# First layer's x loaded a second time in turned form, its low part made by GpSimd; the gate term c turned from a column of v; new placement numbers

## The reference

```python
# layer 0
q, k, v = (proj(Wq, bq), proj(Wk, bk), proj(Wv, bv))
scores = where(adj + eye > 0, q @ k^T / sqrt(32), -inf)
h = x + softmax(scores) @ v @ Wo.T + bo
x = layer_norm(h)
# layer 1
a = x @ w_g[:D];  c = x @ w_g[D:]
scores = Q @ K^T / sqrt(32) + a[:, :, None] + c[:, None, :] + b_g + log(adj + 1e-9)
x = softmax(scores) @ V + x
# layer 2
f = x @ W_fc + b_fc;  logits = leaky(f @ w_q + (f @ w_k)^T + (1 - adj) * -1e9)
x = softmax(logits) @ f + x
# layer 3: as layer 0, with log(max(adj, 1e-8)) added to the scores
```

## Time and profile before

| | before |
|---|---|
| median of 3 runs | 1841.64 us |
| profiled execution | 1840.3 us |
| its span | 1838.4 us |
| TensorE (PE) busy | 1731.4 us (94%), 23564 matmuls |
| VectorE (DVE) busy | 1483.9 us (81%) |
| ScalarE (ACT) busy | 1214.8 us (66%) |
| GpSimd (POOL) busy | 1269.3 us (69%) |
| DMA | 66.46 MB, mean 36 GB/s |
| chain that ended last | PE 77%, DVE 17%, ACT 2% of the span |

### The profile page before, as it was taken

One profiled execution on the slowest core, in us unless ns is written; L12 is line 12 of the kernel. 1 busy time (PEld: TensorE's weight loads), 2 busy tenths in 40 slices (PEclk: granted clock), 3 DMA queues, 4 the chain that ended last, 5 costly groups with the idle time before them and its releaser, 6 DMA issues.

```text
span 1838.4 us, 54870 instructions
## 1 busy us (share of the span) xinstructions
PE 1731.4 (94%) x23564; PEld 1321.4 (72%) x23564; DVE 1483.9 (81%) x3008; ACT 1214.8 (66%) x1894; POOL 1269.3 (69%) x903
## 2 busy tenths in 40 slices
PE   5999998899999999889999999989999999998996
PEld 4677776777777777677777777767777777767774
DVE  5899877777799977877789987787779998777775
ACT  3567765567777676456776777546777676754675
POOL 4443898288964489638895459945888446992788
PEclk8999999999999999999999999999999999999998
DMA  6100010001120000100221000010112100011011
GB/s 166 36 30 13 19 37 25 24 25 53 49 75 19 19 19 31 47 2 25 60 75 43 24 19 19 25 46 8 42 53 71 42 19 18 15 36 35 14 30 36
DMA packets 67734, 66.46 MB, mean 36 GB/s; under 512 B 6051, under 2 KB 67493, under 8 KB 67493
## 3 DMA queue, kind: packets, MB, share of 16 engines
q1 hardware_dynamic: 66388, 62.16, 11.3%
q10 hardware_dynamic: 1104, 0.79, 0.1%
HBM read 54.54 MB, written 8.39 MB: 34 GB/s over the span
## 4 chain that ended last, share of the span: by engine, by line
PE 77%; DVE 17%; ACT 2%; issue 1%; POOL 1%; SPq 1%; DMA 1%; DVEq 0%; POOLq 0%; ACTq 0%
PE gx L609 23%; PE od L747 17%; PE sc L714 17%; PE gx L760 6%; PE gx L634 3%; PE sc L708 3%; PE sc L720 3%; DVE ring L999 3%; PE gx L796 3%; DVE qk L950 2%; PE gx L727 2%; DVE lg L1043 2%; DVE negm L972 1%; DVE parts L972 1%; DVE parts L975 1%
## 5 line engine op out<-in xcount | busy, mean ns | idle before, releaser
L594 POOL TENSOR_TENSOR ring<-ring,adj_c 128x1024 f32<-128x1024 f32 x256 | 609.4, 2406 | 107.7 <-ACT ring L865 55.1
L714 PE MATMUL sc<-qk 32*128 32x256 f32 x9216 | 410.8, 294 | 11.0 <-ACT m_rows L853 4.4
L714 PEld LDWEIGHTS sc<-qk 32*128 32x128 f32 x9216 | 320.5, 184 | 109.3 <-issue 62.7
L850 ACT ACTIVATE aside<-sc 128x1024 f32<-128x1024 f32 x192 | 196.6, 1024 | 232.4 <-PE sc L714 152.7
L865 ACT ACTIVATE ring<-sc 128x1024 f32<-128x1024 f32 x256 | 248.4, 1023 | 29.8 <-PE sc L720 29.3
L569 POOL TENSOR_TENSOR xs<-xs,bo 128x512 f32<-128x512 f32 x96 | 128.3, 1337 | 182.7 <-DVE xt_lo L942 163.5
L747 PE MATMUL od<-ring,vf 128*32 128x256 f32 x3072 | 243.9, 389 | 3.1 <-POOL ring L594 3.1
L747 PE MATMUL od<-ring,ones_r 128*32 128x256 f32 x3072 | 236.7, 380 | 0.0
L972 DVE TENSOR_REDUCE parts<-sc 128x4 f32<-128x1024 f32 x128 | 155.8, 1217 | 50.2 <-PE sc L714 49.5
L999 DVE TENSOR_TENSOR ring<-ring,adj_c 128x1024 f32<-128x1024 f32 x128 | 177.6, 1429 | 0.0
L863 ACT ACTIVATE ring<-sc,vf 128x1024 f32<-128x1024 f32 x128 | 135.8, 1113 | 36.5 <-PE sc L720 36.4
(11 more groups left out here) (146 smaller groups left out, 4433.5 us busy)
## 6 DMA issues: line engine op xcount, KB each, us to landing
adj_c<-in_adj_t SPq DMA_DIRECT2D x96, 256.0 KB, 2.8
adj_r<-in_adj SPq DMA_DIRECT2D x64, 256.0 KB, 3.0
xs<-in_x SPq DMA_DIRECT2D x32, 256.0 KB, 3.1
out<-xs SPq DMA_DIRECT2D x32, 256.0 KB, 2.2
wo<-in_w_o SPq DMA_DIRECT2D x2, 256.0 KB
ring<-in_w_q ACTq DMA_DIRECT2D x1, 256.0 KB, 3.8
ring<-in_w_k ACTq DMA_DIRECT2D x1, 256.0 KB, 4.3
ring<-in_w_v ACTq DMA_DIRECT2D x1, 256.0 KB, 4.6
```

What stands on the lines that cost most here:

```text
L594: pool.tensor_tensor(part, part, adj_c[i.mi % 3][:, t, :].unsqueeze(1).to_broadcast([P, G, N]), ALU.mult).then_inc(weighted, 1)
L714: mm = pe.matmul(sc[:, g, t * N:(t + 1) * N], buf[rows, a, c, t * P:(t + 1) * P], buf[rows, b, c, :], start=(n == 0 and not masked), stop= ...
L850: act.activation(aside[:], sc[:, 0:2, :], ACT.Copy).then_inc(set_aside, 1)
```

## The change

1. **x turned by DMA, layer 0 only.** The host passes `x_t`, the transpose of x. SyncE loads it into two buffers `x_raw` (stage `LT`, 256 KB an item). ScalarE makes `xt_hi` from it, and **GpSimd** makes `xt_lo` = `x_raw` - `xt_hi` (stage `T` in GpSimd's list). The four transposes on TensorE and the subtraction on VectorE are gone in layer 0. x itself is still loaded, for the residual. `XB` of layer 0 now waits for x alone, not for the split.
2. **c from v's column.** GpSimd's `O` now first copies column 257 of v, rounded, and the remainder, into a zeroed `c_pad` (two 128 x 8 instructions). TensorE turns it by two 128 x 128 products with the identity (stage `O`, shaped as `M`), ScalarE copies it to `c_rows`. Gone: six products on TensorE, one VectorE instruction, and the constants `cr_hi`, `cr_lo`, `row_sel`. Scores of item i now wait for V of item i.
3. **New numbers in all tables.** `GAT_START` and `LAST_START` also change, but the order of items stays as it was. `od[0]` and `od[1]` stay two regions.

In the diff the blocks stand in the order SyncE, GpSimd (`T` and `O`), TensorE (`P`, then `O`), ScalarE (`T`).

```diff
 MHA_PLAN1 = {
-    "O": {POOL: [3.4]},
+    "O": {PE: [3.263], ACTE: [3.322], POOL: [-1.904]},
...
-    "P": {PE: [0.888], ACTE: [1.261], DVE: [0.856]},
+    "P": {PE: [0.72], ACTE: [0.977], DVE: [0.737]},
...
+        def x_split(i):
+            return (x0_lo_set, i.i0 + 1) if i.l == 0 else (xt_lo_set, i.k + 1 - i.i0)
...
-            sp.dma_start(xs[:, 0], x_all[items_l0[0].batch]).then_inc(x_loaded[0], 16)
+            sp.dma_start(x_raw[0][:], x_t_all[items_l0[0].batch]).then_inc(xt_loaded[0], 16)
...
+            sp.dma_start(x_raw[1][:], x_t_all[items_l0[1].batch]).then_inc(xt_loaded[1], 16)
             for s, i, c in order[SP]:
-                if s == "LX":
-                    if i.k == 0:
-                        continue
+                if s == "LT" and i.i0 >= 2:
+                    sp.wait_ge(*x_split(items_l0[i.i0 - 2]))
+                    sp.dma_start(x_raw[i.i0 % 2][:], x_t_all[i.batch]).then_inc(xt_loaded[i.i0 % 2], 16)
+                elif s == "LX":
...
+                elif s == "T":
+                    pool.wait_ge(xt_hi_set, i.k + 1)
+                    pool.tensor_tensor(xt_lo[i.k % 2][:], x_raw[i.i0 % 2][:], xt_hi[i.k % 2][:].bitcast(F32), ALU.subtract)\
+                        .then_inc(x0_lo_set, 1)
                 elif s == "O":
+                    gate_c = vf[i.mi % NVF][:, :, D + 1:D + 2].to_broadcast([P, T, G])
+                    pad = c_pad[i.i1 % 2][:].rearrange("p t (g r) -> p t g r", g=G)
                     pool.wait_ge(v_set, v_count(i))
...
+                    pool.tensor_copy(pad[:, :, :, 0], gate_c).then_inc(c_hi_set, 1)
+                    pool.wait_ge(c_hi_set, i.i1 + 1)
+                    pool.tensor_tensor(pad[:, :, :, 1], gate_c, pad[:, :, :, 0].bitcast(F32), ALU.subtract).then_inc(c_pad_set, 1)
...
-                    if s == "P" and i.l == 1:
-                        project(gx_of("ca", i)[:, 0:N], [lambda h: cr_hi[:, h, :], lambda h: cr_lo[:, h, :]],
-                                [lambda h: xh[:, h, :], lambda h: xl[:, h, :]]).then_inc(gx_sem("ca", i), 1)
+                elif s == "O":
+                    pe.wait_ge(c_pad_set, i.i1 + 1)
+                    pe.wait_ge(*gx_emptied("ca", i))
+                    for n in range(T):
+                        mm = pe.matmul(gx_of("ca", i)[:, n * P:(n + 1) * P], c_pad[i.i1 % 2][:, n, :], ident_r[:], start=True, stop=True)
+                    mm.then_inc(gx_sem("ca", i), 1)
...
+                    if i.l == 0:
+                        act.wait_ge(xt_loaded[i.i0 % 2], 16 * (i.i0 // 2 + 1))
+                        if i.k >= 2:
+                            j = items[i.k - 2]
+                            what = "fp1" if j.l == GAT else "vb" if j.l == 1 else "v"
+                            act.wait_ge(gx_sem(what, j), gx_count(what, j))
+                        act.activation(hi, x_raw[i.i0 % 2][:].rearrange("p c n -> p (c n)"), ACT.Copy).then_inc(xt_hi_set, 1)
```

239 lines of the change are left out of this document (113 added, 126 removed).

## The result

The change made the kernel slower: 1895.95 us in the median of 4 runs (1884.13 to 1902.43), beside 1841.02 us (1839.77 to 1842.42) for the kernel before. The ratio is 1.029, 95% interval 1.024 to 1.034. The forecast of 1818 us was wrong in sign, and the loss is larger than that of any rival (C reached to 1879). The profiled execution took 1884.13 us, 43.8 more than the 1840.3 of before, and is the fastest of the four. It also has the highest granted clock, 0.979; the others, at 0.965 to 0.973, took 10 to 18 us more.

A forecast was written before the change was run, and what follows sets the result against it. The prediction took TensorE, busy 94%, as the bound, with VectorE close behind in layer 0 and GpSimd in layer 1. Terms summing to -23.2 took 1840.3 to 1817, and the median's 1.3 gave 1818 us; range 1797 to 1838.

The forecast's parts named there:

- rival C: Layer 0: TensorE waits for x's low part, late in GpSimd's list; slower, 1879 us, partly true about 1846; chance 0.1.
- Transposes: Layer 0, TensorE: four transposes of 0.44 us gone from the chain in each of 32 items, -14.1 us.
- c: TensorE: six products gone -22.4 us, two products turning c +11.8; with GpSimd's lag in layer 1, +8.
- ScalarE's copies stay: Part of the c term: ScalarE's copies remain as before, with no time added for them.
- The lag of GpSimd: Layer 1: two `c_pad` instructions make GpSimd fall behind, 2 us lost a group, +8 us, bounds 0 and +20.
- Low part by GpSimd and the port: Layer 0: GpSimd's new subtraction may collide with VectorE's mask pair at 1.06 us each; +4 us, bounds 0 and +34.
- Layer 0 to 1: Change of layer: an earlier VectorE mask pair shortens TensorE's wait for k's low part; -6 us, bounds -13 and +8.
- Layer 2 to 3: Change of layer: k's low part ahead of two row maxima, 2 us a group saved; -8 us, bounds 0 and -18.
- Layer 3 to 0: Change from layer 3 to the next layer 0: no term in the sum; rival C put its worst wait there.
- Start: Start of the kernel: small parameters issued 5.0 us late behind a new load; +3.5 us, bounds 0 and +6.
- DMA: Whole kernel: 32 more loads of 256 KB, 8.4 MB on 66, cost nothing since the DMA engines are mostly idle.
- Rival B: GpSimd and VectorE take the gain back in layers 1 and 0; 1835 us, 1855 at worst; chance 0.2.

The follow-up runs named there:

- old_lists: The changed kernel with both structural parts but the placement numbers of the kernel before, only new stages getting a place; 1923.85 us, ratio 1.044.
- t_split: old_lists with layer 0's `T` early on GpSimd and ScalarE in the first two items of a group; 1883.85 us, ratio 1.022.
- t_four: t_split with layer 0's `T` early in the first four items of a group instead of two; 1855.2 us, ratio 1.0075.
- u_first: max_slots with VectorE's last small reductions of layer 0's maxima (`U`) moved ahead of the first mask pair; 1835.81 us, ratio 0.9967.
- c_only: The kernel before with only c taken from v's column, old numbers and layer 0's transposes kept; 1844.24 us, ratio 1.0015.
- t_dve: o_late with the low part of layer 0's x made by VectorE instead of GpSimd, `x_t` kept; 1892.7 us, ratio 1.028.
- o_late: The changed kernel with GpSimd's `O` of the first two layer 1 items per group at 0.3 instead of -1.904; 1857.68 us, ratio 1.008.
- max_first: The changed kernel with VectorE's mask pairs of layer 0 placed behind the row maxima; 1872.93 us, ratio 1.017.
- max_slots: o_late plus the move of max_first in the first two layer 0 items of each group alone; 1839.88 us, ratio 0.9986.
- u_later: u_first with its move of `U` made from the fourth item of a group on only; 1837.62 us, ratio 0.9968.

## Why the prediction was wrong

By its own steps, against the profiled executions:

- **Transposes, -14.1.** Right in kind: 17.5 became 17.1 us wherever nothing else waits (old_lists, t_split, t_four, u_first). In the changed kernel itself the beat is 18.0, so the saving never arrives.
- **c, -22.4 + 11.8 + 8 = -2.6.** c_only measured +2 us in all (-0.2 to +5.7 by its interval), so the total is within the forecast's bounds, but not by the steps given. The two `c_pad` instructions cost 0.42 us (0.20 and 0.22), within my bounds. What failed is "ScalarE's copies stay", a term put at nothing: behind `P` the copy had time to run, between the turn and the scores it is waited for, 0.52 us in each item with the old numbers, 16.6 us. The lag of GpSimd that I priced at +8 shows in the changed kernel instead: in layer 1 the chain runs over GpSimd from 697 to 731 us, and the fourth interval (16.2, before 15.3) has GpSimd busy for 16.05 of it. The changed kernel's layer 1 lost 3.1 us a group; c_only has 0.2 of it, and the rest came with the new numbers.
- **Low part by GpSimd and the port, +4 (0 to +34).** Its cost per item was right (1.38 us, expected 1.3 to 1.6), and giving it to GpSimd was right (t_dve). The mis-sized term is the collision. I counted one new operation against one mask pair. What came was that this operation waits 6.5 us for ScalarE and holds `PC` and `PR` back until they, too, meet both pairs: 1.65 us an item on VectorE. The maxima behind the pairs came late by it, and TensorE waited for them. VectorE is busy 17.5 of 18.0 us there and was not the bound by its amount of work, as u_first shows. Steady items cost +0.5 instead of -0.3 us. In the sums over the kernel VectorE has 1479 us where near 1447 was forecast, and GpSimd 1363 where near 1330 was.
- **Layer 0 to 1, -6 (-13 to +8).** The step that failed most. Intervals five and six cost +3.8 us a group and could have given 5: o_late got to 16.9 and 17.9 from before's 17.4 and 22.4. That gain is what I had seen in the new order of VectorE; but I read only VectorE's list there. GpSimd's had `O` a whole stage before V of its item, with the norm behind it. The number stood in the table (-1.904 beside 1.802), and the prediction even says that the norm is queued behind a late `O`, but only for steady layer 1.
- **Layer 2 to 3, -8.** Not there: 86.7 and 86.8 us. The chain now waits at this joint for layer 2's result (L1076), which had stood ahead of the pair of maxima and now stands behind it. I had looked at k alone. This is read from the chain; no run tests it. Layer 3's first three items gained 0.1, 0.1 and 0.6.
- **Layer 3 to 0.** Cost at nothing, since I looked for `T` there (rival C) and found it well placed. The transposes gone from TensorE's list, the q projection became the third user of `gx` behind `F`, and so waited for VectorE's residual sum: +4.7 - 0.4 us, three times, less what layer 3 had gained.
- **Start, +3.5 (0 to +6).** Measured +4.3, and this is luck. The issue times were 12.37 and 20.30 where about 12.3 and 20.3 were worked out, and the first scores came 3.0 us late. But max_first and max_slots have the same issue times and their first `F` at 86.5 and 86.2, ahead of before's 86.8. What is lost by the first `F` is lost behind VectorE's mask pairs and at the lower clock that follows.
- **DMA, 0.** 74.82 MB instead of 66.46, and no wait of it in any chain after the start.
- **The clock.** Not in my sum at all. Behind the pauses of a few us at the joints stand windows at 0.91 and 0.83. In o_late 3.2 of the 8.8 us a group came back by the clock; the pauses themselves gave 5.6, more than the 2 to 4 that its expectation had for them.

Rival B's mechanism (GpSimd and VectorE take the gain back) is there in both layers, with 1.65 us of collision an item of layer 0; rival C's is there in old_lists. What made most of the result, one stage placed too early in GpSimd's list between two layers, was in neither. The range failed because its terms were each taken as independent small losses, though all lie on the same fixed lists, where one misplaced stage costs by what stands behind it.

That the numbers and not the structure lose is shown in so far as the structure with three small moves (u_first) is 0.3% faster than the kernel before (0.2 to 0.4) and 60 us under the change. It is the fastest kernel here that computes everything, with u_later (0.9968) not to be told from it. None reached the forecast's 1818 us. Of the 18 us between, c's term explains 5 and the joint of layers 2 and 3 explains 8. Layer 1 takes 4.5 us a group more than in c_only, and the last four intervals of layer 0 give 5 back; whether one can be had without the other was not found.

## What to carry to other kernels

In a kernel of fixed in-order lists, cost a moved stage by what it waits for and by what stands behind it, on every engine it touches, and do this at each joint of two layers first: there the lists interleave, all engines are near full, and one early place held GpSimd for 19 us. When work goes to GpSimd beside VectorE's two-input operations, the price is not its own length but all GpSimd work that it shifts onto them. And when work is moved closer to its use, cost the copy that now lies between the two: c's six products gave 0.33 us an item and the pause for ScalarE's copy took 0.52 (c_only).
